# A graph-attention kernel: the edge counts of the first stage compared on ScalarE instead of VectorE, and GpSimd's fill of the feature ring moved ahead of its gathers

## The reference, cut to what matters

```python
q = layer_norm(einsum('nf,hfd->hnd', x_node, Wq))      # k and v alike, per node
ke = layer_norm(einsum('ef,hfd->hed', x_edge, Wke))    # ve alike, per edge
rel_k = layer_norm(concatenate([ke, k[:, src]], -1) @ relk_W + relk_b)
qk = sum(q[:, dst] * rel_k, -1) / 4.0
lse = log(segment_sum(exp(qk.T - m[dst]), dst)) + m    # m: segment_max over dst
rel_v = layer_norm(concatenate([ve, v[:, src]], -1) @ relv_W + relv_b)
agg = segment_sum((qk - lse.T[:, dst])[..., None] * rel_v, dst)
z = layer_norm(relu(agg @ z_W + z_b))
out = layernorm(x + z)
```

## Time and profile before

| | us |
|---|---|
| median of 3 runs | 3041.61 |
| lowest and highest run | 3037.26, 3042.23 |
| the profiled execution, its own time | 3035.95 |
| its span, first to last instruction | 3034.2 |

### The profile page before, as it was taken

How to read it: one execution, slowest core, us unless ns; L and a number is a source line. 1 busy time by engine, 2 the same in 40 slices (tenths; PEclk the granted TensorE clock), 3 DMA queues, 4 the chain that set the end, 5 groups by cost and what they waited for, 6 DMA issues and landing times. The chain is left out here.

```text
span 3034.2 us, 76084 instructions
## 1 busy us (share of the span) xinstructions
PE 2840.4 (94%) x18870; PEld 2515.5 (83%) x18870; DVE 2907.3 (96%) x3387; ACT 2306.6 (76%) x5276; POOL 2414.6 (80%) x2622
## 2 busy tenths in 40 slices
PE   4659999999999999999999999999999999997954
PEld 3349999999999999999999999999999999995633
DVE  7879999999999999999999999999999999997947
ACT  2448888888888888888888888888888888885526
POOL 7768888888888888888888888888888888883773
PEclk9889999999999999999999999999999999998977
DMA  3468888888888888888888888888888888886642
GB/s 88 148 188 244 259 255 258 254 257 256 256 258 254 259 256 255 256 256 257 256 256 257 255 257 255 257 254 258 256 255 255 256 257 254 258 263 209 162 122 77
DMA packets 660921, 715.95 MB, mean 236 GB/s; under 512 B 97993, under 2 KB 554430, under 8 KB 660469
## 3 DMA queue, kind: packets, MB, share of 16 engines
q1 hardware_dynamic: 568201, 499.33, 52.4%
q0 software_dynamic: 84896, 211.42, 27.1%
q10 hardware_dynamic: 7756, 4.43, 0.6%
HBM read 482.62 MB, written 231.46 MB: 235 GB/s over the span
## 5 line engine op out<-in xcount | busy, mean ns | idle before, releaser
L1312 POOL DMA_INDIRECT e_rows<-node_table,e_gcol x1564 | 1932.7, 1236 | 422.6 <-issue 306.0
L1132 PE MATMUL banks<-w_edge,e_eat 128*128 128x240 f32 x6256 | 1396.3, 366 | 0.7 <-ACT e_ysq L1241 0.7
L1132 PEld LDWEIGHTS banks<-w_edge,e_eat 128*128 128x128 f32 x6256 | 1188.7, 190 | 89.5 <-issue 1.1
L1125 PE MATMUL banks<-e_h,e_oh 128*128 128x248 f32 x3128 | 805.2, 380 | 3.8 <-DVE e_h L1427 3.6
L1422 DVE TENSOR_REDUCE e_zs<-e_z 128x96 f32<-128x1440 f32 x391 | 638.9, 1634 | 0.2
L1125 PEld LDWEIGHTS banks<-e_h,e_oh 128*128 128x128 f32 x3128 | 534.1, 191 | 37.0 <-DVE e_h L1427 6.4
L1211 ACT ACTIVATE e_agg<-banks 128x496 f32<-128x496 f32 x782 | 453.8, 580 | 90.0 <-PE banks L1125 89.7
L1220 ACT ACTIVATE e_oht<-banks 128x512 bf16<-128x512 f32 x391 | 233.4, 597 | 313.2 <-PE banks L1145 310.8
L1410 DVE TENSOR_TENSOR e_p<-banks,e_yr 128x960 f32<-128x960 f32 x391 | 447.0, 1143 | 4.8 <-PE banks L1132 3.5
L1390 DVE TENSOR_TENSOR e_p<-e_p,e_rows 128x960 f32<-128x960 f32 x391 | 447.0, 1143 | 0.0
L1427 DVE TENSOR_TENSOR e_h<-e_p,e_zw 128x960 f32<-128x960 f32 x391 | 445.8, 1140 | 1.2 <-POOL e_zw L1325 1.2
(11 more groups left out here) (413 smaller groups left out, 2656.4 us busy)
## 6 DMA issues: line engine op xcount, KB each, us to landing
tile_sums<-e_agg SPq DMA_DIRECT2D x391, 496.0 KB
e_q<-q_by_rank SPq DMA_DIRECT2D x1564, 96.0 KB
e_ea<-in_edge_attr SPq DMA_DIRECT2D x390, 256.0 KB
e_rows<-node_table,e_gcol POOLq DMA_INDIRECT x1564
edge_lse<-t_lse_sb SPq DMA_DIRECT2D x14, 448.0 KB, 3.6
edge_qk<-e_qkt SPq DMA_DIRECT2D x130, 48.0 KB
node_table<-n_tb SPq DMA_DIRECT2D x24, 240.0 KB, 2.8
n_x<-in_x SPq DMA_DIRECT2D x24, 128.0 KB, 2.3
```

Source lines behind the costliest of these rows:

```text
L1125: last = nc.tensor.matmul(sums_bank(x, loop, half)[:, (j % 2) * AW:(j % 2 + 1) * AW], oh[:, x % OR, j, :], hh[:, x % HR, j, :, :].rearrang ...
L1132: last = nc.tensor.matmul(out_ps[:, j // 2, (j % 2) * 2 * HC:(j % 2 + 1) * 2 * HC], eat[:, x % 4, j * P:(j + 1) * P], t["w_edge"][:, at:at ...
L1312: g.indirect_dma_start(out=rows[:, k, j, :], out_offset=None, in_=table, in_offset=bass.IndirectOffsetOnAxis(ap=gcol[:, kb, at:at + 1].bit ...
```

## The change

The comparison and the copy of `w_of` leave VectorE. ScalarE's new `compare(k)` makes, for each block of a set, relu(dst + 1 - n), then for the whole set relu(1 - that), which is 1 where dst is less than n and 0 elsewhere; it also copies `w_of`. It stands in ScalarE's turn c after the copy `n_xt` and before the copies L827 and L834, and it waits for the set's gathers. VectorE's `count(k)` keeps the sum and waits for ScalarE (`s_less`). VectorE makes `one_less_n` = 1 - n once, early. The two ring memsets stand ahead of the first gather instead of behind the last.

```diff
@@ gpsimd
             g.memset(zero_s[:], 0.0).then_inc(s_pool2, 1)
+            ring = t["feat"][:].rearrange("p k e -> p (k e)").bitcast(i32)
+            g.memset(ring, 0).then_inc(s_ring, 1)
+            pool.wait_ge(s_ring, 1)
+            g.memset(ring[0:5, :], ONES).then_inc(s_ring, 1)
+            pool.wait_ge(s_ring, 2)
             last_tile = pool.alloc_register("last_tile")
...
-            ring = t["feat"][:].rearrange("p k e -> p (k e)").bitcast(i32)
-            g.memset(ring, 0).then_inc(s_ring, 1)
-            pool.wait_ge(s_ring, 1)
-            g.memset(ring[0:5, :], ONES).then_inc(s_ring, 1)
-            pool.wait_ge(s_ring, 2)
             last_row = pool.alloc_register("last_q_row")
@@ vector
             link(v.tensor_copy(out=n_f[:], in_=n_i[:]))
+            link(v.tensor_scalar(out=n_up[:], in0=n_f[:], scalar1=-1.0, scalar2=1.0, op0=ALU.mult, op1=ALU.add))
...
             def count(k):
                 nb = min(SLOTS, BLOCKS - SLOTS * k)
                 bs = slice(SLOTS * k, SLOTS * k + nb)
-                dve.wait_ge(s_hit[k], 16 * nb)
-                if k >= 1:
-                    dve.wait_ge(s_cnt, k)
-                link(v.tensor_tensor(out=cmp4[:, 0:nb, :], in0=hits[:, bs, 0:P], in1=n_f[:, bs].unsqueeze(2).to_broadcast([P, nb, P]), op=ALU.is_lt))
-                link(v.tensor_copy(out=w_of[:, bs], in_=hits[:, bs, P]))
+                dve.wait_ge(s_less, k + 1)
                 v.tensor_reduce(out=cnt[:, bs], in_=cmp4[:, 0:nb, :], axis=AX.X, op=ALU.add).then_inc(s_cnt, 1)
...
             def sum_rows():
+                dve.wait_ge(s_wof, SETS)
@@ scalar
+            def compare(k):
+                nb = min(SLOTS, BLOCKS - SLOTS * k)
+                bs = slice(SLOTS * k, SLOTS * k + nb)
+                act.wait_ge(s_hit[k], 16 * nb)
+                if k == 0:
+                    act.wait_ge(s_t, len(PICKS))
+                else:
+                    act.wait_ge(s_cnt, k)
+                for i in range(nb):
+                    b = SLOTS * k + i
+                    last = sc_.activation(cmp4[:, i, :], hits[:, b, 0:P], ACT.Relu, bias=n_up[:, b:b + 1], scale=1.0)
+                last.then_inc(s_past, 1)
+                sc_.activation(w_of[:, bs], hits[:, bs, P], ACT.Copy).then_inc(s_wof, 1)
+                act.wait_ge(s_past, k + 1)
+                sc_.activation(cmp4[:, 0:nb, :], cmp4[:, 0:nb, :], ACT.Relu, bias=t["one_c"][:, 0:1], scale=-1.0).then_inc(s_less, 1)
...
                     sc_.activation(xt[:, n % 2, 0:nb, 0:rows], x_ps[:, 0:nb * F].rearrange("p (c n) -> p c n", c=nb)[:, :, 0:rows], ACT.Copy).then_inc(s_xc, 1)
+                for k in SET_AT.get(c, []):
+                    compare(k)
```

More of the change, by code:

```diff
@@ L233, in start @@
     n_f = sb("n_f", [P, BLOCKS])
+    n_up = sb("one_less_n", [P, BLOCKS])
     cmp_room = sb("cmp_room", [P, BLOCKS * KT])
@@ L277, in start @@
                                                 sem("present_summed"), sem("rank_rows_ready"))
+    s_past, s_less, s_wof = sem("dst_past_node"), sem("dst_less_than_node"), sem("first_rank_of_tile")
     s_nrow, s_nf = sem("rank_code_rows"), sem("rank_code_loaded")
```

## The result

| | before | after |
|---|---|---|
| median of 19 runs each, on one chip, us | 3040.24 | 3046.63 |
| lowest and highest run | 3035.91, 3042.85 | 3042.03, 3051.25 |
| ratio, with its 95% interval | | 1.0022 (1.0016 to 1.0028) |
| the profiled execution, its own time | 3035.95 | 3049.33 |
| its span | 3034.2 | 3047.6 |

The changed kernel is slower by 6.4 us, 0.2%. The forecast was 3041.9 with a range up to 3045.5; the time lies above the range. The two profiled executions differ by 13.4 us, twice as much as the medians.

The account below looks back on a forecast made before the run. VectorE and TensorE, busy 96% and 94%, were taken to bound the kernel, nearly all in the edge loop; only the first stage's end would move: +3.2 (ring fill) - 2.9 (`lb`) = +0.3 on 3041.61, so 3041.9 us, range 3034.0 to 3045.5.

Parts of the forecast that it names:

- the second sentence: Whole program: the edge loop is left alone, so the change is worth only the shift of the first stage's end.
- the one on the slow side: Node loop: each set's landing has ScalarE's comparison behind it, nothing regained, +3.2 us, 3044.8; chance 0.16, 0.04 beyond 6.1 us.
- The sum of the first stage: End of the first stage, set by `lb`: +3.2 for the fill, -2.9 for the counting, net +0.3 us.
- The ring fill: Ahead of the gathers: GpSimd's memsets hold up VectorE's copies L547 and L548, delaying the linked chain 3.2 us, bounds 0.6 to 3.4.
- The rival in which that makes the fill cheap: Ahead of the gathers: VectorE's short operations slip between the memsets, delay only 0.6 us, total 3039.3; chance 0.20.
- The pace of the gathers: GpSimd's gathers: without VectorE's `w_of` copies nearly all take 1.01 us, some 1.4 us gained before the last set, bounds 0 to 1.6.
- ScalarE's comparison, about 2.0 us: Node loop: ScalarE's relus and short copy take about 2.0 us per set; sum 3.0 us after the square, two turns 9.1.
- The gain in `lb`, 2.9: Node loop: `lb` comes 2.9 us earlier relative to the start of the gathers, bounds 1.0 to 4.7.
- the drop of turn 8: Node loop: TensorE's granted clock falls to 0.64 between 88.90 and 93.60, costing some 1.6 us; `lb` gains 2.1 with it.
- The rival in which TensorE keeps its clock: Node loop: denser turns keep TensorE at 2.4 GHz, giving 0.8 more in turn 8 and about 2 later, 3039.1; chance 0.12.
- Within 0.2%: Whole kernel: outcome within 6.1 us of the time before, chance 0.90; faster 0.04, slower 0.06.

Follow-up runs that it names:

- i2: The whole change plus 40 more idle instructions on ScalarE, so its edge loop lies 128 further on than in the kernel before; ratio 1.0004 to the kernel before.
- e2: The kernel before with only the comparison moved to ScalarE, the ring fill staying behind the gathers; ratio 1.0003 to the kernel before.
- e1: The kernel before with only the ring fill moved ahead of the gathers, counting still on VectorE; ratio 1.0007 to the kernel before.
- e3: The kernel before with 88 small activations added to ScalarE's list where it is idle; ratio 1.0014 to the kernel before.
- h3: The whole change plus 40 idle instructions on ScalarE, run on a noisy chip; ratio 1.0049 to the kernel before.
- f3: The kernel before with only the comparison moved to ScalarE, plus 40 idle ScalarE instructions, on a noisy chip; ratio 1.0006 to the kernel before.
- g2: The comparison alone on ScalarE plus 40 idle ScalarE instructions, repeated on another noisy chip; ratio 1.0036 to the kernel before.
- h4: The comparison alone on ScalarE plus 40 idle ScalarE instructions, repeated on a third noisy chip; ratio 1.0003 to the kernel before.
- i1: The comparison alone on ScalarE plus 40 idle ScalarE instructions, on a chip like that of the first comparison; ratio 0.9995 to the kernel before.
- f2: The whole change plus 40 idle ScalarE instructions, on a noisy chip; ratio 1.0021 to the kernel before.
- g1: The whole change plus 40 idle ScalarE instructions, repeated on another noisy chip; ratio 1.0043 to the kernel before.

## Why the prediction was wrong

**The step that failed** is the second sentence: the loop over edges, "which the change leaves alone. So the change is worth only what it moves the end of the first stage by". The loop's instructions are the same; their place is not. It cost 5.9 us in the profiled executions and 5.5 by the ratios with and without the transfers, of a miss of 4.7 against the forecast and of 6.4 in all. No rival had it: the one on the slow side reached +3.2, and beyond 6.1 only with a slower comparison on ScalarE, which didn't come.

**The sum of the first stage**, +0.3, is within what i2 leaves to it, +1.2 (-1.5 to +4.0). With the two terms as measured below it is +3.2 - 1.7 = +1.5. Its terms one by one:

*The ring fill, +3.2.* Right in size, and partly by luck: `dst_x` came 3.24 us late, but the waits came at other places. I had the copies L547 and L548 wait for one memset each. It was the cast ahead of them, which used to end within 0.1 of 24.80 where GpSimd now goes on with the fill, and the fill was through before L550 began. VectorE did get in between the two memsets, though: nine operations that are neither copies nor casts ran beside the second one at 0.17 us each, and the copy L549 (0.74 in place of 0.20) met only its end. The rival in which that makes the fill cheap (0.6) fell all the same, since the first memset alone was stood for in full. The rule of the Trainium skill, page "SBUF — State Buffer", section "Who interferes with whom", by which copy and cast forms take a port that GpSimd's instruction holds as a whole, agrees: cast 3.31 and 3.41, the two-input operations beside the second memset 0.17.

*The pace of the gathers.* Right in kind: nearly all take 1.01, and the last one starts 1.6 us later than before although the first starts 3.5 later. That is 1.9 us gained, where I had put 1.6 as the most.

*ScalarE's comparison, about 2.0 us.* Right. Timeline of ScalarE after (answers to the earlier trace rows), and the sum that it releases:

```profile
99.11 0.77 ACT L831 ACTIVATE n_sq<-banks 128x720 f32<-128x720 f32 x1 [1.50 <-PE banks L937]
99.78 0.38 ACT L838 ACTIVATE n_xt<-banks 128x256 f32<-128x256 f32 x1
100.04 1.27 ACT L806 ACTIVATE cmp_room<-room_a,one_less_n 128x128 f32<-128x128 f32 x4
101.21 0.20 ACT L808 ACTIVATE w_of<-room_a 128x4 f32<-128x4 f32 x1
101.34 0.72 ACT L810 ACTIVATE cmp_room<-cmp_room,one_c 128x512 f32<-128x512 f32 x1
...
102.10 0.69 DVE L627 TENSOR_REDUCE cnt<-cmp_room 128x4 f32<-128x512 f32 x1 [1.28 <-ACT cmp_room L810]
...
108.20 0.77 ACT L831 ACTIVATE n_sq<-banks 128x720 f32<-128x720 f32 x1 [1.07 <-PE banks L937]
```

From the square to the sum 102.10 - 99.11 = 3.0 as worked out, and two turns from 99.11 to 108.20 are 9.1 us as worked out.

*The gain in `lb`, 2.9.* Mis-sized. From the first copy `n_xt` of the node loop to `lb` it took 62.05 us before and 60.36 after, a gain of 1.7, and i2 and e2 have 60.0 and 60.4. But e1, which only moves the fill and counts on VectorE, has 59.7: no run shows a gain in `lb` from the comparison on ScalarE itself. Nearly all of the 1.7 is in the last turn, where the blocked copy is gone: the squares of turns 1 and 12 lie 50.67 us apart in both kernels (55.56 to 106.23 and 61.50 to 112.17). The turns of after do come at 3.97 and 5.12 us by turns, where before had 4.76 to 4.86, but what they gain is lost at lower levels of TensorE's clock. The stretch table, columns as in the earlier trace rows, of after:

```profile
79.50:84.50 5.00, 4.43 (x10) 2.55 (x10) 4.46 (x10) 2.42 (x9) 4.07 (x4) 0.66 0.43 115
84.50:90.00 5.50, 3.10 (x12) 1.72 (x10) 3.44 (x7) 5.47 (x17) 4.08 (x4) 1.00 0.45 133
90.00:95.20 5.20, 4.35 (x10) 2.45 (x10) 4.65 (x10) 2.47 (x9) 4.05 (x4) 0.67 0.38 106
```

Twice between turns 1 and 12, in place of the once of the earlier trace rows, TensorE fell from 2.4 towards 1.2 GHz, each time after it had sat idle for VectorE (2.01 us up to 80.07, 2.33 us up to 90.85), and the squares then lay 6.60 and 6.81 us apart; before had one such turn, of 6.50. The prediction weighed whether the drop of turn 8 would stay, and not whether a second could come. That the uneven turns brought it isn't shown: e1 and e3, which count on VectorE as before, had two drops as well, and i2, with the comparison on ScalarE, had one, its squares of turns 1 and 12 lying 49.4 us apart in place of 50.7. The rival in which TensorE keeps its clock fell.

**The remaining 3.5 of the stage end and 3.5 of the tail** in the two profiled executions are for the stage mostly a clock level that differs between executions of one kernel, and for the tail open. The stage: TensorE's first products, which nothing in the change touches, took one time throughout in after, while in before they changed to the shorter one after 44 us. Before, then after, the same two lines of each:

```profile
44.25 0.58 PE L896 MATMUL banks<-bd,colb 128*128 128x120 f32 x2
...
45.48 0.39 PE L896 MATMUL banks<-bd,colb 128*128 128x120 f32 x2
```

```profile
47.49 0.64 PE L914 MATMUL banks<-bd,colb 128*128 128x120 f32 x2
...
49.33 0.64 PE L914 MATMUL banks<-bd,colb 128*128 128x120 f32 x2
```

That put the first `n_xt` 2.8 us later than the chain's 3.24 explain (56.75 for 50.67). The views print a granted clock of 1.00 over both stretches, but that is no reading: the trace's records of the clock begin at 44.6 us in before and at 60.4 in after, and where there is none the view prints 1.00. h3 has records here, and both durations in one execution. Its product, then the stretches of its clock, columns as in the earlier trace rows:

```profile
46.02 0.64 PE L917 MATMUL banks<-bd,colb 128*128 128x120 f32 x2
47.51 0.39 PE L917 MATMUL banks<-bd,colb 128*128 128x120 f32 x2
...
44.50:47.00 2.50, 2.50 (x13) 2.29 (x11) 2.23 (x10) 0.00 (x0) 2.00 (x2) 0.50 0.20 53
47.00:50.00 3.00, 2.96 (x22) 2.53 (x21) 0.42 (x3) 0.00 (x0) 2.09 (x4) 1.00 0.17 44
```

So 0.64 is the product at a granted clock of 0.50, which is 1.2 GHz, and 0.39 at 1.00, which is 2.4 GHz; e3, where it took 0.64 throughout, has 0.50 from 44.5 to 47. The level isn't the kernel's alone: the compare-only kernel with 40 more was profiled four times, and the product took 0.39 in f3 and 0.64 in g2, h4 and i1; the change with 40 more came to 0.39 in f2 and h3 and stayed at 0.64 in g1 and i2. The change as it is stayed at 0.64 in all three of its executions, so a part that is its own isn't ruled out. The tail took 270.3 in i2, whose instructions there are those of after, and 273.8 in e1, whose instructions are all but the fill's place those of before; what makes it 271 or 274 I didn't settle.

**The chances.** "Within 0.2%" had 0.90 and came out just outside, with an interval that reaches inside (1.0016 to 1.0028). The range was made from the terms of one stage; nothing in it stood for the rest of the program, 2840 us of 3034.

## What to carry to other kernels

If an engine's instruction list grows or shrinks ahead of a long loop, compare the number of instruction transfers inside the loop before reading anything else: they were 0 or about 125 here, and with them came 4.5 to 5.9 us that no line of the loop explains. A stop of an engine that the trace puts down to nothing but issue, once a turn and always ahead of the same instruction, is their mark; before a change of ScalarE's list is judged by 6 us, it should be tried with some idle instructions more, so that the loop lies as before modulo 128. And read the granted clock turn by turn in the stretch that is meant to gain, in more than one execution: one or two drops came with either way of counting, and the squares then lay 6.0 to 6.8 us apart in place of about 4.8. Where a trace has no record of the clock, the duration of a product that doesn't change tells the level.

## What the runs showed of the hardware that was not expected

- Instruction transfers in a loop depend on where it lies in ScalarE's list: shifts of 88 and 216 instructions gave 123 to 127 transfers in 2000 us, five a turn, in seven profiled executions; shifts of 0, 48 and 128 none. A transfer carries 8.2 KB. The Trainium skill, page "Runtime: NRT & Kernel Launch", section "Instruction fetch mechanics", says that an engine holds 32 KiB of instructions, that a taken branch to a target outside them has to fetch it before going on, and that the refill goes in blocks of 16 KiB. The first two fit what is seen here: 32 KiB are four pieces of 8.2 KB, a loop that touches four of them and wants the one behind would outgrow that, and ScalarE stops behind each branch back, for up to 3.99 us; that a shorter loop stays inside is argued, not shown. The size of the block doesn't: transfers here are of 8.2 KB, and a shift of 216 behaves as one of 88, which pieces of 256 instructions don't allow.
- The stops of ScalarE are 2.7 us on average, and the pipeline hides all but 0.2 of each: ScalarE waits some 0.8 us there anyway, and as it is busy for 82% of the loop it has time to catch up with most of the rest.
- The first f32 products of TensorE took 0.64 us at a granted clock of 0.50 and 0.39 at 1.00 (h3), and the level they met differed between executions of one kernel; with the longer time came a first `n_xt` 2.8 us later.
- VectorE's durations in a profile are no measure of the loop: the median of the sum `e_zs` is 1632 ns before, 1648 after and 1676 in i2, whose loop is as short as that of before.
- The fill of the ring takes GpSimd 2.65 us for 5 partitions as for 128, and two casts of VectorE stood for it to its end: 0.70 became 3.31, and in e1 the cast of 13 elements took 3.41.
